# Cross-attention and FFN kernel: small statistics operations on GpSimd, batch 2 normalised by two engines, first expert weights split at another place, 40 unused transposes

## Chip, cores and metric

The kernel runs on one core of one Trainium2 chip. The metric is the time of one execution in device microseconds (us). One execution was recorded by the hardware profiler.

## What is computed

```python
# x: (4, 512, 512), f: (4, 512, 512), c: (4, 512, 256); weights of 8 experts
x = x + xattn(layernorm(x), f, c)          # per batch: two int8 SmoothQuant linears
x = x + ffn(layernorm(x), gate_w, w1, b1, w2, b2)

def smooth_quant_linear(x, w):             # x: [T, D], w: [O, D]
    s = sqrt(max(amax_cols(x), eps) / max(amax_cols(w), eps))
    xs, ws = x / s, w * s
    xq, wq = round(xs / x_scale), round(ws / w_scale)   # scales: row maxima / 127
    return xq @ wq.T * x_scale * w_scale.T
xattn: h = smooth_quant_linear(x, f); a = silu(gate) * up; smooth_quant_linear(a, c)

def ffn(h):                                # h: 2048 tokens x 512
    logits = h @ gate_w.T
    sel = top_k(logits.sum(over all tokens), 2)         # two experts for all tokens
    rw = softmax(logits[:, sel])
    y_k = gelu(h @ w1[sel_k] + b1[sel_k]) @ w2[sel_k] + b2[sel_k]
    return sum_k rw_k * y_k
```

## The kernel before

Each engine has its own instruction stream, written out by hand as a list of helper calls, and semaphores between them. There is no planner: the order of the calls in each engine's list is the order of its work. Everything up to about 156 us handles the four batches (512 tokens each, as 4 parts of 128 partitions x 512) in an interleaved manner; after it, 16 pairs of hidden-unit blocks (8 per expert) are worked through, the first one written out (`first_pair`), the others in the same way with Strassen products (`pair`).

The names that the change touches:

- `moments(b, c)` computes mean and variance of batch b for layer norm 1 or 2. On VectorE it is four `bn_stats` (L1183), four `bn_aggr` (L1186) and two small operations on 128 x 4 numbers, `nmean` = -mean (L1188) and `var_e` = var + eps (L1189). VectorE has it for (0, 1), (1, 1), (1, 2), (2, 2), (3, 2); ScalarE has its own form (L882 to L890) for (2, 1), (3, 1), (0, 2).
- `inv_std(b, c)` on GpSimd waits for it, and makes `rstd` = var_e ** -0.5 (L333) and `nmr` = nmean * rstd (L336).
- `normalise` makes x * rstd + nmr: on ScalarE (L866), for batch 2 of norm 2 on GpSimd (L378), and for the second half of batch 3 on VectorE (`normalise_last`, L1300).
- `add_residual` on GpSimd (L373) and `add_last_residual` on VectorE (L1307, the second half of batch 3) add the attention's output, which VectorE's `dequant` (L1260) has written, to `res`.
- `normed2(b, h)` on TensorE transposes the normalised batch, half h, into a PSUM slot `y.b.h` (L630). ScalarE copies it out with token sums (`keep_full`, L932) or without (`keep_summed`, L939; then VectorE's `token_sums`, L1311, has them), and rounds a copy to the high part (`keep_hi`, L944). VectorE takes the difference as the low part (`keep_lo`, L1268).
- `router(b)` on TensorE (L641) multiplies high and low part of batch b with the router's weights; `keep_logits` on ScalarE (L953) copies it out.
- `token_total`, `expert_sums` (TensorE, L651) and `choose_experts` (VectorE, L1323 to L1326) find the two experts. SP waits for `top_ready`, and loads the first `raw1` (w1) and `raw2` (w2).
- `first_weights`: ScalarE rounds the four blocks of raw1 to `a_hi` (`plain_hi`, L956), VectorE makes `a_lo` (L1358). `plain(q, n)` on TensorE (L826) needs them; n = 0 and 1 use batch 0, n = 2 and 3 batch 1. `logit_columns` and `pick_logits` come after `plain(0, 1)`.

The PSUM slots are handed round by the counters `filled` and `drained` (`fill`, `drain`, `emptied`); `y.0.0` is the last use of slot 0 before `first_pair`.

Of the kernel before, what the change touches and what calls it, by code (L numbers as in the profile page):

```python
# [5 lines left out]
ALU = mybir.AluOpType  # L6
# [8 lines left out]
P = 128  # L15
QEPS = 1e-06
QMAX = 127.0
LN_EPS = 1e-05
# [5 lines left out]
def xattn_ffn(  # L24
# [37 lines left out]
    with ExitStack() as ctx:  # L62
# [3 lines left out]
        def sem(name):  # L66
            return ctx.enter_context(nc.semaphore(name))

        def each(name):
            return [sem(f"{name}{b}") for b in range(B)]  # L70
# [15 lines left out]
                      "x2.2 w2.2 x2.3 w2.3").split()  # L86
        SCALES = ("x1.0 w1.0 x1.1 w1.1 w1.2 x1.2 x1.3 w1.3 x2.0 w2.0 x2.1 w2.1 "
                  "x2.2 w2.2 x2.3 w2.3").split()
        SLOTS = [uses.split() for uses in SLOT_USES]
        ALL_DRAINED = [len(uses) for uses in SLOTS]  # L90

# [123 lines left out]
        dve_link = sem("dve_link")  # L215
        pool_link = sem("pool_link")
        gwt_ps, gwt_ready = sem("gwt_ps"), sem("gwt_ready")
        var_ready, rstd_ready, nmr_ready = each("var_ready"), each("rstd_ready"), each("nmr_ready")
        xn_ready, xn2_ready = each("xn_ready"), each("xn2_ready")
        ratio_ready, root_ready, smooth_ready = each("ratio_ready"), each("root_ready"), each("smooth_ready")  # L220
        srow_ready, wmul_ready = each("srow_ready"), each("wmul_ready")
# [2 lines left out]
        xr_ready, wr_ready = each("xr_ready"), each("wr_ready")  # L224
        silu_ready, a_ready, res_added = each("silu_ready"), each("a_ready"), each("res_added")
        hi_ready, lo_ready = each("hi_ready"), each("lo_ready")
        res_last, xn_last = sem("res_last"), sem("xn_last")
        part_ready, tok_ready, t4_sum = each("part_ready"), sem("tok_ready"), sem("t4_sum")
        tsum_ready = [sem(f"tsum_ready{tp}") for tp in range(2)]
        thi_ready = [sem(f"thi_ready{tp}") for tp in range(2)]  # L230
# [87 lines left out]
        def _(pool):  # L318
# [9 lines left out]
            g.affine_select(out=ident[:, :], in_=ident[:, :], compare_op=ALU.not_equal, fill=1.0, base=0,  # L328
                            pattern=[[-1, P]], channel_multiplier=1).then_inc(consts_ready, 1)

            def inv_std(b, c):
                pool.wait_ge(var_ready[b], c)
                g.tensor_tensor(rstd[c - 1][b][:, :], var_e[c - 1][b][:, :], neg_half[:, :], ALU.pow  # L333
                                ).then_inc(rstd_ready[b], 1)
                pool.wait_ge(rstd_ready[b], c)
                g.tensor_tensor(nmr[c - 1][b][:, :], nmean[c - 1][b][:, :], rstd[c - 1][b][:, :], ALU.mult  # L336
                                ).then_inc(nmr_ready[b], 1)

# [35 lines left out]

            def normalise(b):
                pool.wait_ge(nmr_ready[b], 2)
                for j in range(TT):
                    g.tensor_scalar(xv[b][:, j, :], res[:, b * TT + j, :], rstd[1][b][:, j:j + 1], nmr[1][b][:, j:j + 1],  # L378
                                    ALU.mult, ALU.add).then_inc(xn2_ready[b], 1)

# [134 lines left out]
        def _(pe):  # L515
# [84 lines left out]
            def product(b, c, h):  # L600
                n = KD if c == 1 else KI
                for k in range(n // H):
                    emptied(f"xq{c}.{b}.{k}" if c == 1 else f"xq2.{b}")
                    emptied(f"wq{c}.{b}.{k}" if c == 1 else f"wq2.{b}")
                ps, full = fill(f"p{c}.{b}.{h}")
                for j in range(H):
                    at = (H * h + j) * P
                    for k in range(n):
                        last = t.matmul(ps[:, j, :], xq[b][:, k, at:at + P], wq[b][:, k, :],
                                        start=(k == 0), stop=(k == n - 1))  # L610
                last.then_inc(full, 1)
# [9 lines left out]
            def normed2(b, h):  # L621
                ps, full = fill(f"y.{b}.{h}")
                for j in range(TT):
                    if b == B - 1 and j >= H:
                        pe.wait_ge(xn_last, j - H + 1)
                    else:
                        pe.wait_ge(xn2_ready[b], j + 1)
                    for k in range(H):
                        at = (H * h + k) * P
                        last = t.transpose(ps[:, k, j * P:(j + 1) * P], xv[b][:, j, at:at + P], ident[:, :])  # L630
                last.then_inc(full, 1)

            def router(b):
                ps, full = fill(f"r.{b}")
                n = 0
                for h in range(KD // H):
                    pe.wait_ge(lo_ready[b], h + 1)
                    hi, lo = HI_AT[b % 2][h], LO_AT[b % 2][h]
                    for k in range(H):
                        for rows_used, v in ((2 * E, hi), (E, lo)):  # L640
                            last = t.matmul(ps[0:rows_used, 0, :], gwt[:, H * h + k, 0:rows_used],  # L641
                                            xo[b // 2][:, v, k, :], start=(n == 0), stop=(n == 2 * KD - 1),
                                            skip_group_check=True)
                            n += 1
                last.then_inc(full, 1)

            def expert_sums():
                pe.wait_ge(tok_ready, 1)
# [95 lines left out]
            normed2(0, 1)  # L744
            product(3, 2, 0)
            product(3, 2, 1)
            normed2(1, 0)
            normed2(1, 1)
            normed2(2, 0)
            normed2(2, 1)  # L750
            normed2(3, 0)
            normed2(3, 1)
            router(0)
            expert_sums()
            router(1)
            router(2)
            router(3)

            def strassen(p, tp, i, dst, start, first):
                if tp == 0:  # L760
# [70 lines left out]
            def first_pair():  # L831
                for tp in range(2):
                    pe.wait_ge(hid_ready, 8 + 8 * tp)
                    plain(tp, 0)
                    plain(tp, 1)
                    if tp == 0:
                        for b in range(B):
                            logit_columns(b)
                    plain(tp, 2)
                    pe.wait_ge(hid_ready, 8 + 8 * tp + 2)  # L840
                    plain(tp, 3)
                    if tp == 0:
                        pe.wait_ge(w2_ready, 2)
                    down(0, tp, 0, 0, 0, True)
                    down(0, tp, 0, 1, 1, False)
                    last = down(0, tp, 1, 2, 1, True)
                    if tp == 1:
                        last.then_inc(w2_free, 1)
                    down(0, tp, 1, 3, 0, False)
                pe.wait_ge(hid_ready, 8 + 16)  # L850
# [9 lines left out]
        def _(act):  # L860
            s = nc.scalar

            def normalise(b, c):
                act.wait_ge(nmr_ready[b], c)
                for j in range(H if c == 2 and b == B - 1 else TT):
                    s.activation(xv[b][:, j, :], res[:, b * TT + j, :], ACT.Identity, bias=nmr[c - 1][b][:, j:j + 1],  # L866
                                 scale=rstd[c - 1][b][:, j:j + 1]).then_inc(xn_ready[b] if c == 1 else xn2_ready[b], 1)

            sums = [0]

# [70 lines left out]
            def keep_hi(b, h):  # L941
                i, n = place(f"y.{b}.{h}")
                act.wait_ge(drained[i], n + 1)
                s.copy(whole(b // 2, HI_AT[b % 2][h]), part(b // 2, FULL_AT[b % 2][h])).then_inc(hi_ready[b], 1)  # L944
# [98 lines left out]
            normalise(1, 2)  # L1043
            keep_full(1, 0)
            keep_full(1, 1)
            keep_hi(1, 0)
            keep_full(2, 0)
            normalise(3, 2)
            keep_hi(1, 1)
            keep_summed(2, 1)  # L1050
            keep_full(3, 0)
            keep_hi(2, 0)
            keep_logits(0)
            keep_hi(2, 1)
            keep_summed(3, 1)
            keep_hi(3, 0)
            keep_hi(3, 1)
            s.activation(gelu_warm[:, :], half[:, 0:1], ACT.Gelu_apprx_tanh)
            keep_logits(2)
            first_weights()  # L1060
            keep_logits(1)
            keep_logits(3)
            act.wait_ge(raw2_load, 16)
            down_hi(1)
            down_hi(0)

            def gelu(p, i, f, src):
                bias = b1_now[:, f:f + 1]
# [80 lines left out]
        def _(dve):  # L1149
# [25 lines left out]
            def moments(b, c):  # L1175
                if c == 1:
                    dve.wait_ge(x_load[b], 16)
                for j in range(TT):
                    if c == 2 and b == B - 1 and j >= H:
                        dve.wait_ge(res_last, j - H + 1)  # L1180
                    elif c == 2:
                        dve.wait_ge(res_added[b], j + 1)
                    ins = v.bn_stats(stats[b][:, j, :], res[:, b * TT + j, :])  # L1183
                link(ins)
                for j in range(TT):
                    ins = v.bn_aggr(mv[b][:, j, :], stats[b][:, j, :])  # L1186
                link(ins)
                v.tensor_scalar(nmean[c - 1][b][:, :], mv[b][:, :, 0], -1.0, None, ALU.mult)  # L1188
                v.tensor_scalar(var_e[c - 1][b][:, :], mv[b][:, :, 1], LN_EPS, None, ALU.add).then_inc(var_ready[b], 1)  # L1189

            def abs_max(dst, src):
                return v.tensor_reduce(dst, src, AX.X, ALU.max, apply_absolute_value=True)  # L1192
# [285 lines left out]
            choose_experts()  # L1478
            pick_experts()
            keep_lo(2, 1)  # L1480
            keep_lo(3, 0)
            keep_lo(3, 1)
            first_weights()
            pick_bias()
            first_down_weights()
            pick_logits()

# [110 lines left out]
```

## Time and profile before

| | us |
|---|---|
| three timed runs | 827.88, 824.71, 825.21; median 825.21 |
| profiled execution | 823.26, of which the span of the trace is 821.4 |
| TensorE busy | 775.2 (94% of the span) |
| VectorE busy | 487.6 (59%) |
| ScalarE busy | 355.2 (43%) |
| GpSimd busy | 445.9 (54%) |

Busy time is the time in which an engine had an instruction under way; matmuls are pipelined, so a busy TensorE is not one at its peak. The shares are means over two very different parts: up to about 156 us all five engines take turns, from there TensorE works without a break worth naming. The mean granted clock of TensorE over the span was 0.976 of 2.4 GHz.

### The profile page before, as it was taken

What the parts mean: (1) busy time and instruction counts of PE and PEld (TensorE: products, weight loads), DVE (VectorE), ACT (ScalarE), POOL (GpSimd) and SP (SyncE); (2) the same over time, 40 slices, a digit from 0 to 9 for tenths busy, and PEclk for the clock granted to TensorE, in tenths of its full rate; (3) what the DMA queues carried; (4) which work ended last, traced back from release to release, by engine and by line L of the source; (5) the groups of instructions that cost most, each with busy time, mean ns of one, the idle gap of its engine ahead of it and who ended that gap; (6) DMA issues with size and microseconds to landing.
All of it is one profiled execution on the core that took longest, in us unless ns stands there. A gap on an engine that the chain in (4) does not pass through costs nothing.

```text
span 821.4 us, 11341 instructions
## 1 busy us (share of the span) xinstructions
PE 775.2 (94%) x3570; PEld 624.4 (76%) x3577; DVE 487.6 (59%) x693; ACT 355.2 (43%) x660; POOL 445.9 (54%) x473
## 2 busy tenths in 40 slices
PE   5778866999999999999999999999999999999998
PEld 4656543688788888888888888888888888888886
DVE  6999979797754545454545454545454545454545
ACT  3958687733442424242424242424242424242422
POOL 1678898158564646464646464646464646464622
PEclk9799986999999999999999999999999999999999
DMA  9400000301000000000101010101010101000022
GB/s 345 171 1 1 1 1 1 128 1 36 17 27 25 28 24 28 23 28 23 28 23 29 22 30 21 31 20 29 22 32 19 30 21 31 20 31 20 0 103 102
DMA packets 19077, 32.33 MB, mean 39 GB/s; under 512 B 872, under 2 KB 11240, under 8 KB 18160
## 3 DMA queue, kind: packets, MB, share of 16 engines
q1 hardware_dynamic: 18896, 31.98, 11.3%
q8 instruction: 11, 0.18, 0.1%
q10 hardware_dynamic: 160, 0.08, 0.0%
q14 instruction: 10, 0.08, 0.0%
HBM read 27.87 MB, written 4.19 MB: 39 GB/s over the span
## 4 chain that ended last, share of the span: by engine, by line
PE 82%; DVE 9%; POOL 4%; issue 3%; DMA 1%; ACT 1%; ACTq 0%; DVEq 0%; POOLq 0%
PE slot L781 42%; PE slot L768 34%; PE slot L826 3%; DVE rmax L1192 2%; DVE xf L1249 1%; DVE peak_x L1192 1%; POOL res L373 1%; DVE peak_a L1192 1%; DVE xf L1260 1%; DMA b_rows<-in_L_ffn_b 1%; POOL cv L348 1%; DVE stats L1183 1%; POOL rstd L333 1%; POOL h_lo L450 1%; PE slot L563 1%
## 5 line engine op out<-in xcount | busy, mean ns | idle before, releaser
L768 PE MATMUL slot<-xo,a_hi 128*128 128x512 f32 x840 | 259.0, 389 | 0.0
L1513 DVE SCALAR_TENSOR_TENSOR res<-slot,rw,res 128x512 f32<-128x512 f32 x256 | 178.5, 751 | 130.3 <-PE slot L781 130.2
L1542 DVE TENSOR_TENSOR e<-slot,e 128x512 f32<-128x512 f32 x150 | 103.8, 692 | 173.4 <-PE slot L768 173.3
L781 PE MATMUL slot<-w_hi,h_hi 128*128 128x512 f32 x512 | 201.0, 393 | 0.4 <-POOL h_lo L450 0.4
L781 PE MATMUL slot<-w_lo,h_hi 128*128 128x512 f32 x512 | 199.4, 389 | 0.0
L781 PE MATMUL slot<-w_hi,h_lo 128*128 128x512 f32 x512 | 199.3, 389 | 0.0
L768 PEld LDWEIGHTS slot<-xo,a_hi 128*128 128x128 f32 x840 | 157.3, 188 | 33.4 <-DVE e L1542 0.2
L450 POOL TENSOR_TENSOR h_lo<-e,h_hi 128x512 fp32r<-128x512 f32 x96 | 138.2, 1453 | 55.3 <-ACT e L1070 54.3
L768 PE MATMUL slot<-xo,a_lo 128*128 128x512 f32 x420 | 163.4, 389 | 0.0
L781 PEld LDWEIGHTS slot<-w_hi,h_hi 128*128 128x128 f32 x512 | 96.1, 188 | 25.2 <-POOL h_lo L450 5.6
L781 PEld LDWEIGHTS slot<-w_hi,h_lo 128*128 128x128 f32 x512 | 96.1, 188 | 20.2
L450 POOL TENSOR_TENSOR h_lo<-hid,h_hi 128x512 fp32r<-128x512 f32 x32 | 44.1, 1379 | 123.7 <-ACT hid L1070 123.7
L781 PEld LDWEIGHTS slot<-w_lo,h_hi 128*128 128x128 f32 x512 | 96.1, 188 | 19.5
L768 PEld LDWEIGHTS slot<-xo,a_lo 128*128 128x128 f32 x420 | 78.8, 188 | 16.5
L1069 ACT ACTIVATE h_hi<-e,b_now 128x512 fp32r<-128x512 f32 x90 | 65.0, 722 | 57.9 <-DVE e L1542 57.6
L1108 ACT COPY e<-slot 128x512 f32<-128x512 f32 x30 | 17.6, 587 | 164.5 <-PE slot L768 164.5
L464 POOL TENSOR_TENSOR a_lo<-raw,a_hi 128x256 fp32r<-128x256 f32 x45 | 34.5, 767 | 95.9 <-ACT a_hi L959 95.9
L962 ACT CAST w_hi<-raw 128x512 fp32r<-128x512 f32 x32 | 19.8, 623 | 109.7 <-PE slot L781 109.7
L469 POOL TENSOR_TENSOR w_lo<-raw,w_hi 128x512 fp32r<-128x512 f32 x30 | 38.7, 1291 | 50.1 <-ACT w_hi L962 50.1
L1070 ACT ACTIVATE e<-e,b_now 128x512 f32<-128x512 f32 x90 | 63.9, 710 | 0.0
L1069 ACT ACTIVATE h_hi<-slot,b_now 128x512 fp32r<-128x512 f32 x38 | 26.2, 690 | 67.5 <-PE slot L768 56.5
L464 POOL TENSOR_TENSOR a_lo<-ssum,a_hi 128x256 fp32r<-128x256 f32 x60 | 44.0, 743 | 0.0
(145 smaller groups left out, 825.3 us busy)
## 6 DMA issues: line engine op xcount, KB each, us to landing
raw<-in_L_ffn_w SPq DMA_DIRECT2D x32, 512.0 KB, 3.4
res<-in_x SPq DMA_DIRECT2D x4, 1024.0 KB, 11.8
wv<-in_fside_BxS2xS SPq DMA_DIRECT2D x4, 1024.0 KB, 12.7
out_x<-res SPq DMA_DIRECT2D x3, 1024.0 KB, 3.9
cv<-in_ctx SPq DMA_DIRECT2D x4, 512.0 KB, 13.0
out_x<-res SPq DMA_DIRECT2D x4, 256.0 KB, 2.7
b_row<-in_L_ffn_b SPq DMA_DIRECT2D x2, 256.0 KB, 4.6
b_rows<-in_L_ffn_b ACTq DMA_DIRECT2D x1, 64.0 KB, 5.8
```

What stands on the lines that cost most here:

```text
L450: g.tensor_tensor(h_lo[:, i, :], hid[i][:, :], h_hi[:, i, :].bitcast(F32), ALU.subtract).then_inc(h_ready, 1)
L464: g.tensor_tensor(a_lo[:, i, :, :], A_OF[i], a_hi[:, i, :, :].bitcast(F32), ALU.subtract).then_inc(a_ops_ready, 1)
L469: g.tensor_tensor(w2_lo[:, f, :], raw2[:, f, :], w2_hi[:, f, :].bitcast(F32), ALU.subtract).then_inc(w2_ready, 1)
L768: last = t.matmul(dst, a[:, i, k, :], xo[tp][:, v, k, :], start=(start and n == 0), stop=(n == 3 * H - 1), skip_group_check=True)
L781: last = t.matmul(y_bank[j][:, :], a[:, i, j * P:(j + 1) * P], v[:, f, :], start=(start and n == 0), stop=(not start and n == 2), skip_gro ...
L826: last = t.matmul(TILE_BANK[n], a[:, 2 * f + h, k, :], xo[q][:, v, k, :], start=(m == 0), stop=(m == 3 * KD - 1))
L962: s.copy(w2_hi[:, f, :], raw2[:, f, :]).then_inc(w2_hi_ready, 1)
L1069: s.activation(h_hi[:, i, :], src, ACT.Gelu_apprx_tanh, bias=bias).then_inc(hid_ready, 1)
L1070: s.activation(hid[i][:, :], src, ACT.Gelu_apprx_tanh, bias=bias).then_inc(hid_ready, 1)
L1192: return v.tensor_reduce(dst, src, AX.X, ALU.max, apply_absolute_value=True)
L1513: v.scalar_tensor_tensor(out=r, in0=y_bank[j][:, :], scalar=rw[:, ds(p, 1), n:n + 1].rearrange("p a b -> p (a b)"), in1=r, op0=ALU.mult, o ...
L1542: v.tensor_tensor(dst[:, :], src, other[:, :], ALU.add).then_inc(comb_ready, 1)
```

## The change

Five edits, cut to their core:

```diff
+        BN_STATS = ((0, 1), (1, 1), (1, 2), (2, 2), (3, 2))
@@ GpSimd
+            def link(ins):
+                links[0] += 1
+                ins.then_inc(pool_link, 1)
+                pool.wait_ge(pool_link, links[0])
+
             def inv_std(b, c):
                 pool.wait_ge(var_ready[b], c)
-                g.tensor_tensor(rstd..., var_e..., neg_half[:, :], ALU.pow).then_inc(rstd_ready[b], 1)
-                pool.wait_ge(rstd_ready[b], c)
+                if (b, c) in BN_STATS:
+                    g.tensor_scalar(nmean[c - 1][b][:, :], mv[b][:, :, 0], -1.0, None, ALU.mult)
+                    link(g.tensor_scalar(var_e[c - 1][b][:, :], mv[b][:, :, 1], LN_EPS, None, ALU.add))
+                link(g.tensor_tensor(rstd..., var_e..., neg_half[:, :], ALU.pow))
                 g.tensor_tensor(nmr..., nmean..., rstd..., ALU.mult).then_inc(nmr_ready[b], 1)
             def normalise(b):                     # batch 2
-                for j in range(TT):
+                for j in range(H):
@@ VectorE, moments
                 for j in range(TT):
                     ins = v.bn_aggr(mv[b][:, j, :], stats[b][:, j, :])
-                link(ins)
-                v.tensor_scalar(nmean..., mv[b][:, :, 0], -1.0, None, ALU.mult)
-                v.tensor_scalar(var_e..., mv[b][:, :, 1], LN_EPS, None, ALU.add).then_inc(var_ready[b], 1)
+                ins.then_inc(var_ready[b], 1)
@@ TensorE
+                    elif b == 2 and j >= H:       # in normed2
+                        pe.wait_ge(xn_rest, j - H + 1)
+            def keep_clock(use, n):
+                emptied(use)
+                i, _ = place(use)
+                for _ in range(n):
+                    t.transpose(slot[i][:, 0, 0:P], ident[:, :], ident[:, :])
             product(3, 2, 1)
+            keep_clock("y.0.0", 32)
             normed2(1, 0)
             normed2(1, 1)
+            keep_clock("y.0.0", 4)
             normed2(2, 0)
             normed2(2, 1)
+            keep_clock("y.0.0", 4)
             normed2(3, 0)
             ...
             router(2)
-            router(3)
@@ TensorE, first_pair
                     plain(tp, 0)
+                    if tp == 0:
+                        router(3)
                     plain(tp, 1)
@@ ScalarE
+            def normalise_rest(b):
+                act.wait_ge(nmr_ready[b], 2)
+                for j in range(H, TT):
+                    s.activation(xv[b][:, j, :], res[:, b * TT + j, :], ACT.Identity, bias=nmr[1][b][:, j:j + 1],
+                                 scale=rstd[1][b][:, j:j + 1]).then_inc(xn_rest, 1)
             keep_full(1, 1)
+            normalise_rest(2)
             keep_hi(1, 0)
+            normalise(3, 2)
             keep_full(2, 0)
-            normalise(3, 2)
             keep_hi(1, 1)
             keep_summed(2, 1)
             keep_full(3, 0)
             keep_hi(2, 0)
             keep_logits(0)
+            keep_summed(3, 1)
             keep_hi(2, 1)
-            keep_summed(3, 1)
+            s.activation(gelu_warm[:, :], half[:, 0:1], ACT.Gelu_apprx_tanh)
+            first_weights()
             keep_hi(3, 0)
             keep_hi(3, 1)
-            s.activation(gelu_warm[:, :], half[:, 0:1], ACT.Gelu_apprx_tanh)
-            keep_logits(2)
-            first_weights()
             keep_logits(1)
-            keep_logits(3)
             act.wait_ge(raw2_load, 16)
             down_hi(1)
             down_hi(0)
+            keep_logits(2)
+            keep_logits(3)
@@ VectorE
             keep_lo(2, 1)
+            first_weights()
+            pick_bias()
             keep_lo(3, 0)
             keep_lo(3, 1)
-            first_weights()
-            pick_bias()
             first_down_weights()
```

The transposes of `keep_clock` turn the identity matrix and write it to a PSUM slot that nobody reads before it is overwritten.

## Rows read from the trace of the kernel before

**Rows 1.** The page, first line.

```profile
span 821.4 us, 11341 instructions
```

**Rows 2.** The chain that ended last, 116 to 162 us: start, us, engine, tile, line.

```profile
149.65 0.18 DVE sum_row L1323
...
153.64 2.14 PE slot L641 x8
...
156.04 5.70 PE slot L826 x24
```

**Rows 3.** The same chain, 11 to 20 us.

```profile
11.30 0.17 DVE nmean L1188
...
18.04 1.78 DVE peak_x L1192 x2
```

**Rows 4.** VectorE's timeline: start, us, operation, out<-in, count, idle time before.

```profile
125.43 1.31 DVE L1188 TENSOR_SCALAR nmean<-mv 128x4 f32<-128x4 f32 x1
...
127.88 2.71 DVE L1260 SCALAR_TENSOR_TENSOR wv<-slot,scale,wsc_row 128x512 f32<-128x512 f32 x4
130.51 2.46 DVE L1183 BATCH_NORM_STATS2 stats<-res 128x6 f32<-128x512 f32 x4
...
133.57 1.29 DVE L1307 TENSOR_TENSOR res<-res,wv 128x512 f32<-128x512 f32 x2
...
148.17 1.22 DVE L1268 TENSOR_TENSOR xo<-xf,xo 128x1024 fp32r<-128x1024 f32 x1
...
155.51 1.43 DVE L1358 TENSOR_TENSOR a_lo<-raw,a_hi 128x256 fp32r<-128x256 f32 x4 [0.89 <-ACT a_hi L956]
...
158.00 0.29 DVE L1352 TENSOR_REDUCE b_col<-picked 128x16 f32<-128x128 f32 x1
```

**Rows 5.** GpSimd's timeline, 115 to 142 us, the fourth row from 137.7 to 138.4 us.

```profile
115.89 0.23 POOL L359 TENSOR_SCALAR scale<-rmax 128x4 f32<-128x4 f32 x1
...
121.74 7.42 POOL L373 TENSOR_TENSOR res<-res,wv 128x512 f32<-128x512 f32 x6
129.13 1.01 POOL L333 TENSOR_TENSOR rstd<-var_e,neg_half 128x4 f32<-128x4 f32 x1
...
137.78 1.84 POOL L378 TENSOR_SCALAR xf<-res,rstd,nmr 128x512 f32<-128x512 f32 x1
139.58 1.97 POOL L333 TENSOR_TENSOR rstd<-var_e,neg_half 128x4 f32<-128x4 f32 x1
```

**Rows 6.** VectorE's timeline, 139.1 to 139.8 us.

```profile
138.97 1.71 DVE L1268 TENSOR_TENSOR xo<-xf,xo 128x1024 fp32r<-128x1024 f32 x1
```

**Rows 7.** TensorE's timeline, 118 to 147 us.

```profile
120.52 1.04 PE L580 MATMUL slot<-ident,xf 128*128 128x128 f32 x8
...
125.09 1.67 PE L609 MATMUL slot<-xf 128*128 128x512 bf16 x7
131.41 4.43 PE L630 MATMUL slot<-ident,xf 128*128 128x128 f32 x16 [4.64 <-ACT xf L866]
...
142.82 3.87 PE L630 MATMUL slot<-ident,xf 128*128 128x128 f32 x16 [0.76 <-ACT xf L866]
```

**Rows 8.** ScalarE's timeline, 130 to 156 us.

```profile
130.45 2.94 ACT L866 ACTIVATE xf<-res,nmr,rstd 128x512 f32<-128x512 f32 x4 [1.53 <-POOL nmr L336]
...
145.13 0.59 ACT L932 ACTIVATE xf<-slot 128x512 f32<-128x512 f32 x1
...
146.28 1.04 ACT L944 CAST xo<-xf 128x1024 fp32r<-128x1024 f32 x1
...
155.07 1.32 ACT L956 CAST a_hi<-raw 128x256 fp32r<-128x256 f32 x4
```

**Rows 9.** Busy time by stretch, then TensorE's granted clock, the DMAs' share, GB/s.

```profile
120.00:130.00 10.00, 6.29 (x43) 4.33 (x41) 9.88 (x18) 8.92 (x16) 10.00 (x11) 1.00 0.01 2
...
130.00:131.00 1.00, 0.00 (x0) 0.00 (x0) 1.00 (x2) 0.55 (x1) 0.92 (x3) 0.57 0.00 0
```

**Rows 10.** DMA issues by line, 151.0 to 151.6 us: KB each, us to landing.

```profile
raw<-in_L_ffn_w SPq DMA_DIRECT2D x1, 512.0 KB, 3.7
```

More of the change, by code:

```diff
@@ L217, in xattn_ffn @@
         gwt_ps, gwt_ready = sem("gwt_ps"), sem("gwt_ready")
-        var_ready, rstd_ready, nmr_ready = each("var_ready"), each("rstd_ready"), each("nmr_ready")
+        var_ready, nmr_ready = each("var_ready"), each("nmr_ready")
         xn_ready, xn2_ready = each("xn_ready"), each("xn2_ready")
@@ L226, in xattn_ffn @@
         hi_ready, lo_ready = each("hi_ready"), each("lo_ready")
-        res_last, xn_last = sem("res_last"), sem("xn_last")
+        res_last, xn_last, xn_rest = sem("res_last"), sem("xn_last"), sem("xn_rest")
         part_ready, tok_ready, t4_sum = each("part_ready"), sem("tok_ready"), sem("t4_sum")
@@ L329, in _ @@
                             pattern=[[-1, P]], channel_multiplier=1).then_inc(consts_ready, 1)
+            links = [1]
+            def link(ins):
+                links[0] += 1
+                ins.then_inc(pool_link, 1)
+                pool.wait_ge(pool_link, links[0])
             def inv_std(b, c):
                 pool.wait_ge(var_ready[b], c)
-                g.tensor_tensor(rstd[c - 1][b][:, :], var_e[c - 1][b][:, :], neg_half[:, :], ALU.pow
-                                ).then_inc(rstd_ready[b], 1)
-                pool.wait_ge(rstd_ready[b], c)
+                if (b, c) in BN_STATS:
+                    g.tensor_scalar(nmean[c - 1][b][:, :], mv[b][:, :, 0], -1.0, None, ALU.mult)
+                    link(g.tensor_scalar(var_e[c - 1][b][:, :], mv[b][:, :, 1], LN_EPS, None, ALU.add))
+                link(g.tensor_tensor(rstd[c - 1][b][:, :], var_e[c - 1][b][:, :], neg_half[:, :], ALU.pow))
                 g.tensor_tensor(nmr[c - 1][b][:, :], nmean[c - 1][b][:, :], rstd[c - 1][b][:, :], ALU.mult
@@ L1186, in moments @@
                     ins = v.bn_aggr(mv[b][:, j, :], stats[b][:, j, :])
-                link(ins)
-                v.tensor_scalar(nmean[c - 1][b][:, :], mv[b][:, :, 0], -1.0, None, ALU.mult)
-                v.tensor_scalar(var_e[c - 1][b][:, :], mv[b][:, :, 1], LN_EPS, None, ALU.add).then_inc(var_ready[b], 1)
+                ins.then_inc(var_ready[b], 1)
             def abs_max(dst, src):
```

## Prediction

> **What bounds the kernel now.** I read the page's first line, then the chain of waits, then the timelines of the five engines from 95 to 172 us. The profiled execution has a span of 821.4 us [rows 1] and a time of 823.26 us, so 1.86 us lie around the span; the median of the three timed runs is 825.21 us, 1.95 us more. All sums are differences against the profiled execution, and I add them to the median.
>
> From 156 us on, TensorE runs one matmul behind the other (24 in 5.70 us [rows 2]), and nothing in the change touches that loop. So the change can only move the moment at which the second expert product, `plain(0, 1)`, starts: 156.04 + 5.70/2, less the tail of a matmul, is 158.86. Before it the end is set by a relay: GpSimd adds residuals, VectorE takes the statistics, GpSimd turns them into factors for batches 1, 2 and 3, all engines normalise batch 3, TensorE transposes it, the token sums pick the expert (149.65 [rows 2]), SP loads its weights, ScalarE and VectorE split them, and TensorE starts. The load is issued at 151.27 and lands 3.7 us later [rows 10]; ScalarE's first split starts at 155.07 [rows 8]. Call that moment z. VectorE's part follows at 155.51 [rows 4] and TensorE starts at z + 0.97.
>
> **Statistics on GpSimd, batches 0 and 1 at the start.** VectorE drops two small operations (0.17 us, 0.08 apart [rows 3]), GpSimd gets two of about 0.23 us (the row of `scale`, of the same shape [rows 5]). Per batch the factors come 0.1 to 0.3 us later, VectorE is free 0.16 us earlier. The first path runs through ScalarE and TensorE back to VectorE at 18.04 [rows 3]. Bounds: -0.2 to +0.3 us; I take +0.1.
>
> **Statistics on GpSimd, batches 1, 2 and 3 at 125 us.** In batch 1 the two small operations hold VectorE for 2.45 us: `nmean` takes 1.31 us at 125.43 and `var_e` ends only as the `dequant` starts at 127.88 [rows 4], against 0.17 us for one at the start [rows 3]. GpSimd then runs six residual additions of 1.24 us back to back [rows 5], and each of VectorE's two operations ends at one of their boundaries. The other direction shows too: GpSimd's fourth normalisation takes 1.84 us where its neighbours start 0.76 apart, VectorE's second `keep_lo` takes 1.71 instead of 1.22 [rows 6], and GpSimd's power takes 1.97 instead of 1.01 [rows 5]. So two such operations exclude each other, and they take turns. (The Trainium skill, "SBUF — State Buffer", Who interferes with whom, says the same of VectorE instructions with two SBUF inputs or in a two-port mode and GpSimd: "the other fully blocks". It speaks against this change, because it holds for whatever VectorE does next as well. By the rule, what comes back is the schedule below; without it, batch 1's 2.45 us would be all gain.)
>
> Now the hand schedule. VectorE is free at 125.41; `dequant(3, 2, 0)` must wait for the product that TensorE starts at 125.09 [rows 7], so it starts at 126.15, and four of 0.68 [rows 4] end at 128.85 instead of 130.59: 1.75 gained. Four `bn_stats` take 2.46 and the aggregation 0.4: 131.7 instead of 133.4. GpSimd comes to `inv_std(1, 2)` at 129.13 [rows 5] and now needs 0.45 longer, so the factors are there at 130.85, and `add_residual(3, 0)` runs from there, 1.24 each. VectorE's `add_last_residual` is issued at 131.7, into the middle of it; before it ran alone at 133.57 in 1.29 [rows 4]. In turns: GpSimd to 132.1, VectorE to 132.75, GpSimd to 134.0, VectorE to 134.6. Then GpSimd's four operations for batch 2 (0.2 + 0.2 + 1.0 + 0.2, and two waits of 0.08) end at 136.2; before, 135.4. That is where the gain goes. VectorE's statistics of batch 3 are ready at 137.4 (137.9 before).
>
> **Batch 2 normalised by two engines.** GpSimd does two parts, 136.3 to 137.8, and saves two, which were 2.6 us long because the last was blocked (137.78 and 1.84 [rows 5]). ScalarE takes the others: two of 0.73 [rows 8]. It is free from `keep_full(1, 1)` at 136.6, ends at 138.05, and only then does `keep_hi(1, 0)`, to 139.05. VectorE's `keep_lo(0, 0)` is issued at 137.4 and gets its turn at 137.8, to 138.95; GpSimd's `nmean` of batch 3 waits for it, and then `keep_lo(1, 0)`, possible from 139.05, takes the next turn, to 140.5. The power runs 140.6 to 141.6 and batch 3's factors are ready at 141.9, where they were before (139.58 + 1.97 + 0.28 [rows 5]). If `keep_hi(1, 0)` is 0.7 late, the power goes first but the last product waits for `keep_lo(1, 0)` instead: 141.8 again. Without any exclusion it would be 139.4. Bounds: 139.4 to 142.6; I take 141.9.
>
> **40 transposes.** One costs 0.11 us at the full clock (8 start to start, 1.04 us with the tail) and 0.23 at half (16 in 3.87) [rows 7]. The first 32 stand behind `product(3, 2, 1)`, which ends at 126.8, and before batch 1's transposes, which start at 131.41 [rows 7]: 3.5 us, to 130.3, hidden; at half the clock they would be 7.4 and end at 134.2. The granted clock was 1.00 from 120 to 130 and 0.57 in the slice from 130 to 131 [rows 9], after TensorE had been idle since 126.8. So it should stay at 2.4 GHz longer. Is that worth anything? Batch 3's 16 transposes could end up to 1.9 us earlier than 146.69 [rows 7]; but the new order has ScalarE do `keep_full(2, 0)` (1.15 [rows 8]) behind the normalisation, so `keep_full(3, 0)` ends at 147.6 (146.3 before), and VectorE's queue reaches the last token sum at 146.7 as before. Token total: 147.9 (148.1). Then `keep_lo(2, 0)` waits for `keep_hi(2, 0)` until 148.55 and ends at 149.75; before it started at 148.17 and ran 1.22 [rows 4]. Experts: +0.1 (between -0.5 and +0.5). The eight later transposes cost 0.45 twice in waits of over 1 us: nothing.
>
> **First weights in another place.** ScalarE is now ready at 152.5, so z is the landing alone: 154.97 + 0.1 + 0.1 = 155.17. It was the landing before too, nearly (154.97 against 155.07), so this reordering gains at most 0.1. What it costs is behind it. `router(3)` took 2.14 us in a wait (153.64 to 155.78, just ahead of 156.04 [rows 2]); now it stands between `plain(0, 0)` and `plain(0, 1)`, where TensorE has no other wait. And it needs `keep_lo(3, 1)`, which VectorE does last: a_lo from z + 0.44 for 1.43, `pick_bias` until z + 3.22 (158.00 + 0.29 [rows 4]), `keep_lo(3, 0)` until z + 4.45, `keep_lo(3, 1)` until z + 5.65. TensorE ends `plain(0, 0)` at z + 3.8, does the first half of the router at z + 4.6, waits, and ends the second half (0.95, half of the eight) at z + 6.75. `plain(0, 1)` starts there instead of at z + 3.79: **+3.0 us**. ScalarE's `keep_logits(3)` and the GELUs behind it, the logit columns, `pick_logits` and GpSimd's power all move by the same 3 us and stay as far ahead of the down products as they were.
>
> **Sum.** +0.1 (start) +0.1 (experts) +3.0 (router) = +3.2 us: 826.5 for a profiled execution, **828.4 us** as median. Between 0.5 us and 4.6 us slower from the terms' own bounds around this case, without the rivals: 825.7 to 829.8.
>
> **Rivals.** (1) The lead survives: GpSimd's power for batch 3 isn't blocked and its factors come at 139.9 instead of 141.9. For it: a shift of 0.6 us in ScalarE's `keep_hi(1, 0)` decides the turn. Against: worked through twice, another turn takes its place. z is then 2.0 earlier, the router still costs 3.0: +1.1, 826.3 us. (2) Faster: besides that, batch 3's transposes at 2.4 GHz pull the token sums and ScalarE's queue forward by another 1.9 to 2.4, so z comes 4.4 earlier; from z = 152.1 on it outweighs the router. Net -1.3 or better, 823.9 us. Against: ScalarE's `keep_full(2, 0)` in between. (3) Slower by over 0.5%: the 32 transposes run at half the clock or start late, and hold batch 1's transposes from 131.4 to 134.2; from a start later than 127.9 at the full clock, or with any half-clock stretch longer than 1 us, they decide. +2.6 on top: 831.0 us. For it: the clock was at 0.5 in many stretches with gaps. Against: it was 1.00 from 120 to 130 [rows 9]. (4) The transposes don't hold the clock, which falls in the gap before batch 3: the forecast's time, within 0.4, since ScalarE and VectorE bound that stretch.
>
> **Chances.** Forecast, with (4) in it, 0.47; (1) 0.2; (2) 0.13; (3) 0.2. A difference under 0.5% (4.1 us) can't be told from none here. Of the forecast's share a quarter lies above 829.3, of (3) nearly all; below 821.1 lies half of (2). So: faster 0.07, within 0.63, slower 0.3. The range goes from 822.8 (most of (2)) to 831.2.
>
> **What would show it.** `nmean` on GpSimd and `dequant(3, 2, 0)` at 126.2; `add_last_residual` over 2.5 us long around 132 to 134.6; batch 2's factors after 136; ScalarE idle near 140 to 142; `max_index` at about 150.3; ScalarE's first a_hi within 0.2 us of the landing; a gap and then `router(3)` on TensorE after `plain(0, 0)`, and 6.7 us from z to `plain(0, 1)`. The forecast is wrong if the landing moves by more than 1 us, or if `keep_lo(3, 1)` is done before `plain(0, 0)` ends.

## The result, and the profile after

The changed kernel takes 827.85 us (median of 14 runs) where the kernel before takes 825.05 us (14 runs): ratio 1.0033, 95% interval 1.0022 to 1.0044, or +2.8 us (1.8 to 3.6). It is slower by a third of a percent, within the 0.5% that were called no change. The forecast was +3.2 us. The profiled execution took 827.31 us with a span of 825.5 us, 4.05 us more than the one before.

The page's first line and its row of granted clocks; the clock's mean over the span went from 0.976 to 0.983, and the kernel still got slower:

```profile
span 825.5 us, 11428 instructions
...
PEclk9899979999999999999999999999999999999999
```

The chain that ended last, changed kernel, 141 to 166 us: start, us, what. It answers to [rows 2]:

```profile
141.96 0.39 POOL nmr L345
142.38 1.52 ACT xf L887 x2
143.90 0.67 ACT xf L959 x3
144.56 0.29 issue
144.85 0.20 ACT xf L959
145.10 3.03 PE slot L641 x16
148.13 2.41 PE slot L652 x8
150.55 0.81 PE slot L668 x8
151.38 0.18 DVE sum_row L1349
...
153.00 3.33 DMA raw<-in_L_ffn_w
156.35 0.41 ACT a_hi L983
...
159.72 1.23 DVE xo L1294
160.95 0.14 issue
161.09 2.13 PE slot L652 x8
163.22 2.74 PE slot L845 x12
```

Three things are to be seen. `router(3)` (L652, 161.09) now stands behind the landing of the weights, with VectorE's `keep_lo(3, 0)` (L1294, 159.72) ahead of it; before, it ended just ahead of the first product. The call that its second half needs, `keep_lo(3, 1)`, follows at once and ends at 162.08 (the two are one row, x2, in VectorE's timeline below). z, ScalarE's first a_hi, is 156.35 instead of 155.07. And there is a wait that the prediction did not have: TensorE's transposes of batch 3 (L641) begin at 145.10, 2.8 us after the factors, released by ScalarE's L959, that is by `keep_full(2, 0)`.

VectorE and GpSimd, changed kernel, the rows that answer to [rows 4, 5]:

```profile
126.18 0.38 DVE L1214 BATCH_NORM_AGGREGATE mv<-stats 128x2 f32<-128x6 f32 x4
127.13 2.73 DVE L1286 SCALAR_TENSOR_TENSOR wv<-slot,scale,wsc_row 128x512 f32<-128x512 f32 x4 [0.57 <-PE slot L618]
...
132.56 3.11 DVE L1333 TENSOR_TENSOR res<-res,wv 128x512 f32<-128x512 f32 x2
...
141.06 1.23 DVE L1294 TENSOR_TENSOR xo<-xf,xo 128x1024 fp32r<-128x1024 f32 x1 [1.48 <-ACT xo L971]
...
159.72 2.36 DVE L1294 TENSOR_TENSOR xo<-xf,xo 128x1024 fp32r<-128x1024 f32 x2
```

```profile
130.29 0.24 POOL L342 TENSOR_SCALAR nmean<-mv 128x4 f32<-128x4 f32 x1
...
132.18 2.94 POOL L382 TENSOR_TENSOR res<-res,wv 128x512 f32<-128x512 f32 x2
135.21 0.56 POOL L342 TENSOR_SCALAR nmean<-mv 128x4 f32<-128x4 f32 x1
...
140.84 1.04 POOL L344 TENSOR_TENSOR rstd<-var_e,neg_half 128x4 f32<-128x4 f32 x1
141.96 0.38 POOL L345 TENSOR_TENSOR nmr<-nmean,rstd 128x4 f32<-128x4 f32 x1
```

VectorE's stall of 2.45 us is gone (0.57 us of idle time, the wait for the product), and what it gave is spent right away: `add_last_residual` takes 3.11 us instead of 1.29, and GpSimd's `nmean` for batch 2 0.56 instead of 0.24.

To compare executions, the span is cut at four instructions: r, the factors of batch 0 for norm 2 (the end of GpSimd's `nmr`); the factors of batch 3; z; the first of the logit columns, two expert products after z. b3 stands for the factors of batch 3, cols for the first of the logit columns. All is in us and worked out from the timelines of the profiled executions, one for each line; the ratio is that of the timed runs to the kernel before, and 0.0010 of it is 0.8 us:

```
kernel                          r       b3 - r   z - b3   cols - z  span - cols   ratio to before, 95%
before                        119.95    21.88    13.24     6.60      659.7        -
changed                       121.07    21.27    14.01     9.55      659.6        1.0033, 1.0022 to 1.0044
changed, again        (e12)   122.31    22.14    13.95     9.53      660.0        1.0041, 1.0029 to 1.0054
changed, bias late    (e11)   120.38    21.50    13.90    10.07      660.0        1.0032, 1.0020 to 1.0043
changed, weights back  (e1)   121.48    22.15    14.44     6.60      659.6        1.0014, 1.0000 to 1.0027
changed, full2 first   (e3)   119.96    22.01    12.15    10.02      659.7        1.0026, 1.0012 to 1.0039
changed, no transposes (e4)   122.16    21.48    12.79    10.07      659.9        1.0048, 1.0032 to 1.0064
before + weights       (e2)   119.44    21.81    12.64    10.07      659.6        1.0038, 1.0023 to 1.0053
before + stats, all    (e5)   122.47    23.53    12.99     6.60      659.6        1.0021, 1.0006 to 1.0035
before + stats, norm 2 (e8)   120.90    23.49    13.03     6.61      659.8        1.0018, 1.0005 to 1.0031
before + stats, (1,2)  (e6)   121.68    21.70    12.57     6.61      659.7        0.9998, 0.9987 to 1.0008
best                   (e7)   122.00    20.72    13.20     6.62      659.8        0.9972, 0.9960 to 0.9985
best, no transposes    (e9)   122.07    20.10    14.08     6.62      659.7        0.9979, 0.9967 to 0.9991
best, last first      (e10)   120.89    20.07    13.09     6.60      660.0        0.9965, 0.9952 to 0.9977
```

The last stretch is the same for all, as the prediction had it. `cols - z` takes two kinds of values and nothing between: 6.6 with the old places of the first weights and the router, 9.5 to 10.1 with the new ones. r differs by 1.2 us between two executions of one kernel (changed, changed again), and `z - r`, too, by 0.8 (35.3 and 36.1). So the 4.05 us between the two profiled executions hold some 1 us of scatter, and the medians' 2.8 us are the better size. A difference of under 1 us in r or `z - r` between two single profiles shows nothing by itself.

### The profile page after: what moved, and what is told of

It is laid out like the page before. It is cut to its first block, busy times and chain, and to the rows that moved or that the text cites. A ratio compares the mean times of both kernels' runs of the same rounds, so it can differ in the third digit from the quotient of the medians.

```text
span 825.5 us, 11428 instructions
## 1 busy us (share of the span) xinstructions
PE 776.5 (94%) x3617; PEld 625.7 (76%) x3617; DVE 487.1 (59%) x683; ACT 356.6 (43%) x662; POOL 446.5 (54%) x481
## 4 chain that ended last, share of the span: by engine, by line
PE 80%; DVE 9%; POOL 5%; issue 3%; DMA 1%; ACT 1%; SPq 0%; ACTq 0%; DVEq 0%; POOLq 0%
PE slot L800 42%; PE slot L787 33%; PE slot L845 2%; DVE rmax L1218 2%; POOL res L382 2%; DVE peak_x L1218 1%; DVE xf L1286 1%; DVE xf L1275 1%; DVE peak_a L1218 1%; DMA b_rows<-in_L_ffn_b 1%; DVE clip L1233 1%; POOL cv L357 1%; POOL rstd L344 1%; POOL h_lo L459 1%; PE slot L652 1%
```

## Experiments

**e1 and e2: the place of the first weights, undone and alone.**

```diff
 # e1, against the changed kernel (ScalarE's and VectorE's orders go back too)
             router(2)
+            router(3)
                     plain(tp, 0)
-                    if tp == 0:
-                        router(3)
                     plain(tp, 1)
```

> The changed kernel with one edit undone: the places of the first weights, pick_bias, keep_hi and keep_lo of batch 3, keep_logits and router(3) are those of before. Theory A (the router behind the first expert product costs 3 us, the rest little): 2.9 us faster than the changed kernel, so within 1 us of the kernel before; z (ScalarE's first a_hi) within 0.5 us of the changed kernel's 156.35, and plain(0, 1) starts at z + 3.8 instead of z + 6.7. Rival (the relay before the landing is what got slower, and the router stands in a wait that is there anyway): under 1 us faster than the changed kernel, z + 6 or more.

> The kernel before with this one edit alone (first weights and router(3) in the new places). Theory A: +2.9 us against the kernel before (ratio 1.0035), z where it was or 0.1 earlier, plain(0, 1) at z + 6.7. Rival: under +1 us.

e1: 826.12 us, ratio 1.0014; 1.6 us below the changed kernel by the ratios, less than the 2.9 expected (from the two intervals, an estimate, 0.2 to 3.0), and 1.2 us above the kernel before, just over the 1 us expected. `cols - z` is 6.60 as expected (2.95 less), but z came late, 158.06, so that the expected "within 0.5 us" failed: z - r is 36.6 instead of 35.3. Of the 1.3 us, 0.9 stand in the landing (157.64, 36.16 after r instead of 35.26; the changed kernel's second profile has 36.06), and 0.4 in ScalarE, which in this order was still at `keep_logits(2)` when the weights landed.

e2: 826.66 us, ratio 1.0038 or +3.1 us (1.9 to 4.4), +2.9 expected: right, though z came 0.7 earlier against r than in the kernel before, and not 0.1. So this edit alone makes a slowdown of the forecast's size, while undoing it leaves 1.2 us (0 to 2.2): that the other edits come to nothing together isn't shown by time. e2's trace shows why `cols - z` is 10.07 there. The chain, 151 to 165 us:

```profile
151.51 1.09 PE slot L641 x4
152.60 2.25 issue
154.85 4.57 PE slot L825 x12
159.42 1.85 PE slot L641 x8
161.27 2.76 PE slot L825 x12
```

`plain(0, 0)` (L825, 154.85) takes 4.57 us, `plain(0, 1)` the same twelve matmuls in 2.76. TensorE idled 2.25 us ahead of it, since the router that stood there is gone. The granted clock, 1.00 until then, was 0.81 in the stretch from 155 to 156 us and 0.50 from 156 to 159.

**e3: ScalarE empties y.2.0 ahead of normalising batch 3.**

```diff
-            normalise(3, 2)
             keep_full(2, 0)
+            normalise(3, 2)
```

> The changed kernel with keep_full(2, 0) ahead of normalise(3, 2) on ScalarE again. In the changed kernel TensorE's transposes of batch 3 wait for the PSUM slot that keep_full(2, 0) empties, and begin at 145.10 though batch 3's factors are there at 142.34. Theory B (this slot is what delays the landing by the 1.3 us seen): transposes of batch 3 begin 0.9 us after the factors, end 1.5 to 2 us earlier, z is 1.0 to 1.6 us earlier, time 826.5. Rival (the token sums are bound by ScalarE's and VectorE's queues, as the prediction had it): the transposes begin earlier, z moves by under 0.4 us, time as the changed kernel's.

825.88 us, ratio 1.0026. Theory B held in the trace, but not in the time (1.3 us less expected, 0.6 measured). TensorE's timeline, e3:

```profile
142.10 1.06 PE L662 MATMUL slot<-ident 128*128 128x128 f32 x4
142.96 3.05 PE L641 MATMUL slot<-ident,xf 128*128 128x128 f32 x16
```

The transposes begin 1.0 us after the factors (141.97) instead of 2.8, and `z - b3` is 12.15 against 13.90 to 14.01 in the three executions with the changed kernel's order, 1.8 us earlier where 1.0 to 1.6 were expected. The first product gave 0.5 of it back (`cols - z` 10.02): the clock fell here too, behind a gap of 2.26 us. The time's intervals overlap, so the 0.6 us between the ratios are not shown by time alone.

**e4: without the transposes.** The three `keep_clock` calls are left out.

> The changed kernel without its 40 unused transposes. Theory: TensorE's clock falls near 131 instead of 136, batch 1's 16 transposes run at half the clock (2 us longer, behind ScalarE), keep_full(1, 1) ends about 0.5 us later, z is 0 to 0.8 us later; time within 0.8 us of the changed kernel's. Rival (the transposes are worth their while, they hold the clock into the router): 2 us or more slower than the changed kernel. Second rival (they stand in the way): 1 us or more faster.

828.24 us, ratio 1.0048; the changed kernel has 1.0033 and, taken again, 1.0041. That is no difference beyond the intervals. The second rival, that the transposes stand in the way, is out: the kernel did not get faster without them. In the trace `z - b3` is 1.2 us shorter and `z - r` 1.0, where z was expected 0 to 0.8 us later, and the clock fell at 134.3 us, not near 131. Over all fourteen executions that fall came between 134.2 and 141.5 us in the seven with the transposes, and between 128.3 and 134.3 us in the seven without. What that is worth in time stays open here.

**e5, e8, e6: the statistics alone, for five, three and one of the batches**, each on the kernel before.

```diff
+        BN_STATS = ((0, 1), (1, 1), (1, 2), (2, 2), (3, 2))   # e5; e8: the last three; e6: (1, 2)
-                link(ins)
+                if (b, c) in BN_STATS:
+                    ins.then_inc(var_ready[b], 1)
+                    return
+                link(ins)
```

> The kernel before with the statistics' small operations on GpSimd for all five pairs, nothing else. Theory (the prediction's): +0.1 to +1 us from batches 0 and 1 at the start; around 130, add_last_residual and add_residual(3, 0) take turns (add_last_residual's two over 2.5 us instead of 1.3), batch 2's factors come 0.8 us later relative to batch 1's product, and the landing moves by no more than 0.5: +0.3 to +1.5 us in all. Rival (the 2.45 us of VectorE's stall come back): 1.5 us or more faster than the kernel before.

> The same for layer norm 2 alone: (1, 2), (2, 2), (3, 2); batches 0 and 1 of norm 1 keep theirs on VectorE. Theory: 0.3 to 1.2 us faster than with all five pairs, so within 0.5 us of the kernel before; the first clip at 21.4 to 22 us instead of 22.1 to 23. Rival (the start's shift seen in the traces is scatter from execution to execution): no difference to the one with all five.

> The same for (1, 2) alone, the one batch whose small operations were blocked on VectorE. Theory: batch 2's and 3's factors come 0.5 us earlier each than with all of norm 2, since GpSimd's four operations in a row are two again; VectorE's stall is gone, but the two residual additions still take turns: 0 to 1 us faster than the kernel before. Rival (GpSimd's extra operations cost nothing): as with all of norm 2.

826.58, 825.85 and 824.20 us: ratios 1.0021, 1.0018, 0.9998. The rival of e5 falls: the stall does not come back as time. But two expectations failed as well: in e5 `z - r` grew by 1.4 us where the landing was to move by 0.5 at most (the time, +1.7 us, is just over the 1.5 expected), and e8 is 1.5 us above the kernel before and not within 0.5. The step is between e8 and e6, 0.0020 or 1.6 us (the intervals overlap a little; `z - r` is 36.5 and 34.3), not between e5 and e8: what costs is giving GpSimd batches 2 and 3; batch 1 alone is even with the kernel before. GpSimd's timeline of e5, and then of e6:

```profile
137.21 0.23 POOL L343 TENSOR_SCALAR var_e<-mv 128x4 f32<-128x4 f32 x1
...
138.95 5.03 POOL L387 TENSOR_SCALAR xf<-res,rstd,nmr 128x512 f32<-128x512 f32 x4
144.07 0.24 POOL L342 TENSOR_SCALAR nmean<-mv 128x4 f32<-128x4 f32 x1
```

```profile
132.76 2.50 POOL L382 TENSOR_TENSOR res<-res,wv 128x512 f32<-128x512 f32 x2
135.21 1.47 POOL L344 TENSOR_TENSOR rstd<-var_e,neg_half 128x4 f32<-128x4 f32 x1
...
137.07 4.09 POOL L387 TENSOR_SCALAR xf<-res,rstd,nmr 128x512 f32<-128x512 f32 x4
141.13 1.97 POOL L344 TENSOR_TENSOR rstd<-var_e,neg_half 128x4 f32<-128x4 f32 x1
```

The four normalisations of batch 2 last 5.03 in e5 and 4.09 in e6; e8 has 5.03 as well. With 0.6 us more of GpSimd's own operations for each batch, `b3 - r` is 23.5 in e5 and e8, 21.7 in e6 and 21.9 before. At the start, the first batch's factors come at 13.36 to 13.52 us in the seven executions with `(0, 1)` on GpSimd and at 12.94 to 13.10 in the seven without: +0.4 us, each against each.

**e7, e9, e10: the faster version.** Statistics on GpSimd for (1, 2) alone, batch 2 by two engines, the transposes, `keep_full(2, 0)` first, first weights and router where they were. e9 leaves out the transposes, e10 exchanges two calls on VectorE:

```diff
             keep_lo(0, 0)
-            keep_lo(1, 0)
             normalise_last()
+            keep_lo(1, 0)
```

> What the experiments so far point to: statistics on GpSimd for (1, 2) alone, batch 2 normalised by two engines, the 40 transposes, keep_full(2, 0) ahead of normalise(3, 2), first weights and router(3) in their old places. Theory: batch 3's transposes begin 0.9 us after its factors, z 12.2 us after them (13.2 before), plain(0, 1) at z + 3.8: 1 to 2.5 us faster than the kernel before (822 to 823.3). Rival (ScalarE, loading its table and rounding batch 3 ahead of the weights, bounds z as soon as the landing is earlier): under 0.7 us faster.

> The faster version (e7) without the 40 unused transposes. Theory (the clock they hold is worth up to half a us of ScalarE's keep_full and no more): 0 to 1 us slower than e7's 822.12. Rival (they pay for themselves, as leaving them out of the changed kernel suggested, 0.4 to 2.4 us): over 1 us slower. Second rival (without them TensorE is free earlier): faster than e7.

> e7 with normalise_last ahead of keep_lo(1, 0) on VectorE, so that GpSimd's last product of batch 3 no longer takes turns with keep_lo(1, 0). Theory (the two engines exclude each other for such operations): the product takes 0.2 us instead of 0.82, batch 3's factors come 0.6 us after the power's end less 0.5, z 0 to 0.5 us earlier, because keep_lo(1, 0) is done later and VectorE's queue to the last token sum is 0.5 to 1 us longer: within 0.7 us of e7. Rival (the factors are the whole path): 0.6 us or more faster than e7.

e7: 822.12 us, ratio 0.9972: 2.3 us faster than the kernel before, as expected. But its `z - b3` is 13.20 and not 12.2: the weights landed at 155.29, and ScalarE, which does the table, the GELU and `keep_logits(2)` before them, was free at 155.92. So the rival's mechanism is there, for 0.6 us of it, and its size was off. In the trace the gain stands in `b3 - r` (20.72, 1.2 less than before); the rest of the 2.3 us isn't located. The edit that makes it is most likely batch 2 by two engines: e9 is e6 with that edit alone, its ratio is 0.0019 (1.6 us) lower, though the intervals overlap a little, and its `b3 - r` is 20.1 where e6 has 21.7.

e9: 822.98, ratio 0.9979: 0.6 us slower, inside the interval; its factors came 0.6 us earlier and its token total 0.9 us later against them. e10: 822.20, ratio 0.9965, the lowest; it and e7 are the same within their intervals. GpSimd's last product of batch 3, e7 and then e10:

```profile
139.91 1.91 POOL L344 TENSOR_TENSOR rstd<-var_e,neg_half 128x4 f32<-128x4 f32 x1 [0.98 <-DVE var_e L1219]
141.90 0.82 POOL L345 TENSOR_TENSOR nmr<-nmean,rstd 128x4 f32<-128x4 f32 x1
```

```profile
138.77 1.91 POOL L344 TENSOR_TENSOR rstd<-var_e,neg_half 128x4 f32<-128x4 f32 x1 [0.97 <-DVE var_e L1219]
140.76 0.20 POOL L345 TENSOR_TENSOR nmr<-nmean,rstd 128x4 f32<-128x4 f32 x1
```

0.82 becomes 0.20 as soon as `keep_lo(1, 0)` isn't there to take its turn. That is the exclusion shown. `z - r` fell by 0.76 us, more than the theory's 0.5, but not by the way that was thought: the factors came 0.65 us earlier, and VectorE's last token sum, whose queue had got longer as the theory had it, only 0.06 (it ended 26.84 us after r in e7 and 26.78 in e10), the landing 0.15. The other 0.6 us are ScalarE's: in e10 it was free 0.3 us ahead of the landing, in e7 0.6 behind it.

**e11: pick_bias behind keep_lo.**

```diff
             first_weights()
-            pick_bias()
             keep_lo(3, 0)
             keep_lo(3, 1)
+            pick_bias()
```

> The changed kernel with pick_bias behind keep_lo(3, 0) and keep_lo(3, 1) on VectorE. Theory (of the router's 3.0 us, 2.0 are its own matmuls and 1.0 is the wait for keep_lo(3, 1)): keep_lo(3, 1) ends at z + 4.6 instead of z + 5.65, plain(0, 1) starts at z + 5.7 to 5.9 instead of z + 6.7 and the logit columns at z + 8.6; 0.9 us faster than the changed kernel. Rival (the wait is the clock's or the logits', not keep_lo's): plain(0, 1) at z + 6.5 or later.

827.66 us, ratio 1.0032: no faster, and `plain(0, 1)` started at z + 7.2, as the rival had it, `cols - z` 10.07. `keep_lo(3, 1)` did end at z + 4.67, as expected, instead of z + 5.73, but TensorE wasn't there. TensorE's granted clock by stretch (the number after POOL's), changed kernel and then e11:

```profile
156.00:157.00 1.00, 0.00 (x0) 0.00 (x0) 0.21 (x1) 0.65 (x3) 0.00 (x0) 1.00 1.07 416
...
158.00:159.00 1.00, 1.00 (x6) 0.79 (x5) 0.93 (x4) 1.00 (x2) 0.00 (x0) 1.00 0.73 277
159.00:160.00 1.00, 1.00 (x6) 0.75 (x4) 0.83 (x3) 1.00 (x3) 0.00 (x0) 1.00 0.48 105
```

```profile
155.00:156.00 1.00, 0.00 (x0) 0.00 (x0) 0.00 (x0) 0.22 (x1) 0.00 (x0) 1.00 1.05 353
...
158.00:159.00 1.00, 1.00 (x4) 0.81 (x3) 0.91 (x1) 1.00 (x3) 0.00 (x0) 0.54 0.46 155
159.00:160.00 1.00, 1.00 (x3) 0.72 (x3) 1.00 (x2) 1.00 (x4) 0.00 (x0) 0.50 1.00 326
```

Both idled 1.8 us ahead of the first product. In e11 the clock then went to 1.2 GHz (0.54 and 0.50), the product took 4.1 us, and the wait for `keep_lo` was covered by it. So how far 3.0 us split into router and wait isn't shown by e11; it shows that the split depends on the clock.

**e12: the changed kernel again.**

> The changed kernel once more, on the same chip as the three others. Theory (the place of the front, up to the residual addition near 100 us, moves by 1 us from one execution to the next with TensorE's clock, and the rest follows): its first residual addition starts anywhere from 99 to 102 us, and from there the distances are those of the first profile within 0.6 us; ratio 1.003 again. Rival (the front's 1.1 us belongs to the statistics of batches 0 and 1): 100.3 to 100.6 again.

829.14 us (6 runs), ratio 1.0041; first residual addition at 101.73 (100.45 in the first profile), so the theory holds for the front. Its distances are the first profile's but for `b3 - r`, 0.87 more, which is over the 0.6 expected.

## Why the prediction was right

**What bounds.** Right: nothing behind the logit columns changed (659.6 to 660.0 in all 14 executions), and only the start of the second product counted.

**Router and first weights, +3.0.** Right in way and size: +3.1 us alone (e2), 2.95 in the trace. The steps came as written: z + 0.97 for the first product, `keep_lo(3, 0)` done at z + 4.6 (forecast z + 4.45), `keep_lo(3, 1)` at z + 5.73 (z + 5.65), `plain(0, 1)` at 163.06, z + 6.71 (z + 6.75). The gain on the other side was put at 0.1 at most and was more: with the new order z came 0.02 to 0.03 us behind the landing in all six executions, with the old one 0.4 to 0.6 in six of eight (0.1 in the kernel before, 0.02 in e10). Missed was a second price: the router had also kept TensorE busy ahead of z. In four of six executions with the new order (e2, e3, e4, e11) the clock fell to 1.2 GHz in the product behind the gap, and `cols - z` was 10.0 to 10.1 instead of 9.5: another 0.5 us. In the eight executions of the old order that gap was 0.26 us at most, and the clock did not fall there.

**The stall of 2.45 us that isn't a gain.** Right: there is no gain in e5, and in the changed kernel batch 2's factors came 0.9 us later against r (16.39, before 15.46), forecast 0.8. Batch 3's factors were forecast 21.95 after r (141.9 less 119.95), and came at 21.3 to 22.2 in four executions of this order. That sum has two halves which cancel: the statistics alone put them 1.6 us later (e5), and batch 2 by two engines takes about as much back (e6 and e9, above). By turns `keep_lo(1, 0)` went ahead of the power (e1, where GpSimd's `var_e` took 1.29) or behind it (changed kernel).

**Batch 3 to the landing, +0.1.** The sum was nearly right, the way was not. The prediction had the transposes of batch 3 follow their inputs, though it had written down the moved `keep_full(2, 0)`. That call empties the slot which `y.3.0` takes next, so they waited until 145.1: 1.8 us in TensorE's queue, shown by e3. `z - b3` was forecast as 13.3 and is 13.9 to 14.0. The prediction counted the ScalarE time of the moved call and not the slot that hung on it. That z - r is near the forecast all the same (35.3 and 35.4 in two executions, forecast 35.1; 36.1 in the third) is in part luck: in the first two the factors came 0.4 to 0.7 us ahead of the forecast.

**Start, +0.1.** Too small: the factors come 0.4 us later, outside the stated +0.3, since GpSimd's two operations start 0.3 us apart and don't overlap, where VectorE's start 0.08 apart. In time it can't be told (e5's 1.0021 against e8's 1.0018).

**Transposes, 0.** Right within what time can tell (e4, e9). They ran at 127.7 in 3.66 us, hidden, and the clock held to 135 instead of 130; then it fell all the same. Rival (3), that they stand in the way, is refuted: they ended 1.85 us before the next transposes started. Rivals (1) and (2), that the relay's lead survives, are refuted for this order: they need z at 33.1 and 30.7 us after r, and it came at 35.3 to 36.1. (1) was near for another order: e7 has 33.9, e10 33.2.

**The sum.** Part of the agreement is luck. In the traces the start (0.4), `z - r` (0.2 and 1.0) and `cols - z` (2.95) add up to 3.5 to 4.3 us, and the medians differ by 2.8; which part is smaller in the timed runs isn't shown. One of the prediction's own signs of being wrong came up, too: the landing moved by more than 1 us, from 154.96 to 156.33. Of these 1.4 us, 1.1 stand ahead of r, where two executions of one kernel differ by as much. The sign should have been counted from r; there the landing moved by 0.3 us (by 1.1 in e12). And the stated bounds don't add up to the stated 0.5 to 4.6 us: those of the start, the experts and batch 3's factors around 3.0 give -0.2 to +4.5.

## What to carry to other kernels

Work moved out of a wait isn't saved, it has to be done somewhere: ask whether the new place has a wait as well (the router's had none, 3.0 us), and what the engine does in the old one afterwards (TensorE idled, and the clock fell in four of six). When a call that empties a buffer is moved, follow the buffer, not only the caller's queue. When two engines exclude each other for some operations, a stall taken off one of them is worth only what its next such operation does not give back; move the one that was blocked (e6), and leave those that were not.

## What the runs showed of the hardware

VectorE's residual additions, which have two SBUF inputs, and GpSimd's alternated, one instruction each: in the changed kernel GpSimd's ended at 133.45 and 135.13, VectorE's at 134.00 and 135.68, and VectorE's two took 3.11 us where they took 1.29 alone. But a GpSimd operation does not always hold VectorE up for the whole of its time. The Trainium skill ("SBUF — State Buffer", Who interferes with whom) says that whichever of the two issues first has the shared ports for the whole instruction; in the changed kernel GpSimd's power (140.84 to 141.88) was under way when VectorE's `keep_lo(1, 0)` started at 141.06 and ran its free 1.23 us, while in e6 the power took 1.97 behind a `keep_lo` that had begun. There the measurement decides: a power that had begun did not hold VectorE up.

A gap of 1.8 us on TensorE, behind some 4 us of router matmuls, was followed by a fall to 1.2 GHz in one execution and not in two others with the same gap (1.82; 1.81 and 1.79 us); gaps of 2.13, 2.25 and 2.26 us were followed by it in e4, e2 and e3. The twelve matmuls behind it took 4.1 us in the one (e11); behind the gap of 2.25 us in e2 they took 4.57, against 2.76 at 2.4 GHz.
